# Self-loops counted per node in the setup of a four-layer graph network, and four gathers per tile instead of five

## What is computed

```python
src = concatenate([_s, _d, arange(12500)]); dst = concatenate([_d, _s, arange(12500)])   # then sorted by dst
# layer 0, four steps: a = segment_sum((feat @ W[k].T + b[k])[etype, src], dst); feat = gru(a, feat)
# layer 1, twice:      h = mlp(x + segment_sum(x[src], dst))
# layer 2:             out = segment_sum((x @ W)[src] * deg^-.5[src] * deg^-.5[dst], dst) + b; batch norm
#                      (with one more self-loop per node, added by the layer itself)
# layer 3:             rst = x @ Wself.T + mean over edges of (x[src] * weight) @ Wneigh.T + biases
```

## Time and profile before

| | us |
|---|---|
| median of 3 runs | 9373.61 |
| lowest and highest | 9371.31, 9383.71 |
| the profiled execution | 9385.09 |
| its span, first to last instruction | 9383.3 |
| its mean granted clock | 0.879 |

### The profile page before, as it was taken

The page is one execution under the profiler, slowest core; times in us unless marked ns, Lnnn a source line. Parts: engine busy times, 40 slices in busy tenths (PEclk is TensorE's granted clock), DMA queues, the critical chain, the costliest instruction groups (busy, mean ns, idle before and its releaser), DMA issues.

```text
span 9383.3 us, 311202 instructions
## 1 busy us (share of the span) xinstructions
PE 7002.6 (75%) x128691; PEld 5978.8 (64%) x128692; DVE 7411.2 (79%) x16871; ACT 2629.0 (28%) x6519; POOL 5105.8 (54%) x4469
## 2 busy tenths in 40 slices
PE   3666666668888887887777777756578777748988
PEld 2333333348877887887777676655567766637887
DVE  7888888869988997887888766555567766668998
ACT  0000000013333332333555433311133322224443
POOL 0000000026667776776666588777778867755554
PEclk8887787879999999999999888877888888869999
DMA  3211111147777777777666777777777777748888
GB/s 87 66 46 46 46 47 51 46 130 205 203 209 205 208 207 205 206 203 209 179 176 179 201 211 211 216 217 203 222 214 205 206 225 212 209 117 228 225 225 193
DMA packets 1186021, 1618.18 MB, mean 172 GB/s; under 512 B 421509, under 2 KB 864808, under 8 KB 1181691
## 3 DMA queue, kind: packets, MB, share of 16 engines
q1 hardware_dynamic: 916698, 898.54, 35.7%
q10 hardware_dynamic: 126656, 482.46, 15.0%
q0 software_dynamic: 141280, 217.70, 11.4%
HBM read 1034.03 MB, written 564.09 MB: 170 GB/s over the span
## 4 chain that ended last, share of the span: by engine, by line
issue 32%; DVE 23%; PE 18%; POOL 14%; DMA 7%; DVEq 5%; ACT 1%; SPq 0%; ACTq 0%; POOLq 0%
POOL work L910 14%; DMA work<-node_rows,work 5%; DVE work L1916 4%; DVE work L1891 4%; PE ps_agg L1142 3%; DVE hs L1882 2%; PE ps_pair L1089 2%; PE ps_gate L1186 2%; DVE work L1872 2%; PE ps_agg L1120 1%; PE ps_agg L1122 1%; PE ps_agg L1121 1%; DVE work L1911 1%; DVEq L1898 1%; PE ps_gate L1188 1%
## 5 line engine op out<-in xcount | busy, mean ns | idle before, releaser
L910 POOL DMA_INDIRECT work<-node_rows,work x4410 | 5049.1, 1145 | 2197.8 <-issue 1408.1
L1142 PE MATMUL ps_agg<-work 128*128 128x64 bf16 (+1 forms) x29400 | 1152.6, 197 | 769.4 <-DMA work<-node_rows,work 693.7
L1120 PE MATMUL ps_agg<-work 120*128 120x64 bf16 (+1 forms) x12544 | 1433.2, 201 | 249.4 <-DVE work L1916 241.0
L1142 PEld LDWEIGHTS ps_agg<-work 128*128 128x128 bf16 x29400 | 1039.1, 101 | 825.0 <-issue 753.1
L1121 PE MATMUL ps_agg<-work 120*128 120x64 bf16 x12544 | 1426.9, 201 | 17.6 <-issue 17.3
L1122 PE MATMUL ps_agg<-work 120*128 120x64 bf16 x12544 | 1427.2, 201 | 11.1 <-issue 11.1
L1120 PEld LDWEIGHTS ps_agg<-work 120*128 120x128 bf16 x12544 | 1240.8, 104 | 287.2 <-issue 286.0
L1121 PEld LDWEIGHTS ps_agg<-work 120*128 120x128 bf16 x12544 | 1228.8, 104 | 27.0 <-issue 13.9
L1122 PEld LDWEIGHTS ps_agg<-work 120*128 120x128 bf16 x12544 | 1223.6, 103 | 9.7 <-issue 9.4
L1089 PE MATMUL ps_pair<-rows_now,work 128*128 128x64 bf16 x26112 | 1040.8, 200 | 133.7 <-DMA work<-src_onehots 55.3
L1911 DVE TENSOR_TENSOR work<-work 120x1024 f32<-120x1024 f32 x784 | 955.6, 1219 | 188.1 <-DMA work<-bounce_f 187.7
(11 more groups left out here) (323 smaller groups left out, 12115.4 us busy)
## 6 DMA issues: line engine op xcount, KB each, us to landing
bounce_f<-work ACTq DMA_DIRECT2D x816, 480.0 KB
work<-bounce_f SPq DMA_DIRECT2D x784, 480.0 KB
work<-src_onehots SPq DMA_DIRECT2D x918, 256.0 KB
bounce<-work ACTq DMA_DIRECT2D x102, 727.5 KB
work<-bounce SPq DMA_DIRECT2D x98, 727.5 KB
work<-node_rows,work POOLq DMA_INDIRECT x4410
work<-grid_vals SPq DMA_DIRECT2D x49, 960.0 KB, 5.0
node_rows<-stage SPq DMA_DIRECT2D x686, 48.0 KB
```

Of the source, the lines that this page charges most:

```text
L910: pool.indirect_dma_start(out=ring[:, at.slot3() * LB + b, 0:3 * H], out_offset=None, in_=table_of(at.p), in_offset=bass.IndirectOffsetOnA ...
L1120: mm(acc[:, to:to + n], hot, low[at.two()][0:ROWS, b, 0:n], start=b == 0, stop=False)
L1142: last = mm(acc[:, k * TYPE_W:k * TYPE_W + n], hot, ring[:, u * LB + b, x * H:x * H + n], start=False, stop=end and p < P_GIN1 and k == K ...
```

## The change

Self-loops no longer go into the grid or the left-over batches. In the setup each edge record carries a mark for a self-loop (in `PEN`, negative), and such edges get neither a slot nor a left-over place. GpSimd makes for each of them a row of flags by type, weight and its three parts (`own_fields`); the placing matmul of the left-over rows sums them per node as a fifth record behind four batches (`RECS` = 5 records, `LB` = 4 batches, so the matmul keeps its width of 35), and GpSimd folds the sums (`own_sums`): counts for four types, the sum of weights, and the count plus one. In the passes `take_sums` adds count times own row: in passes 0 to 3 per type, in 4 to 7 with the count plus one (which replaces the identity matmuls), in 8 with the weight sum. SP waits for `sum_taken` before it reloads a record slot or `rows_now`, as both are now read there. GpSimd issues four gathers per tile; their batches are four on TensorE too. In `rank_pair` several pairs of small VectorE instructions become one over both tiles.

```diff
-LB = 5
+LB = 4
 LEFT = LB * P
+RECS = LB + 1
...
         def load_recs(at, more):
+            if not (isinstance(at.i, int) and at.base + more < 6):
+                sp.wait_ge(sum_taken, at.tiles(more - 5))
+                sp.sem_inc(sp_ran, 1)
...
             if p < P_GCN:
                 sp.wait_ge(tile_summed, NT * p + CREDIT_T + 6 * CHUNK)
+                sp.wait_ge(sum_taken, NT * p + 6 * CHUNK)
                 reload(p, 5)
             store_rows(At(p, NT - 1))
             if p < P_GCN:
                 sp.wait_ge(tile_summed, NT * (p + 1) + CREDIT_T)
+                sp.wait_ge(sum_taken, NT * (p + 1))
                 reload(p, 6)
...
+        def own_fields(q, par):
+            two, to = win[par], left_now[:, :, :, LB, :]
+            pool.wait_ge(own_known, q + 1)
+            pool.sem_inc(pool_ran, 1)
+            g.tensor_scalar(own_here, own, 0.0, None, ALU.is_lt)
+            for k in range(K):
+                g.tensor_scalar(own_type[:, :, :, k], two[:, :, :, TYPE], float(k), None, ALU.is_equal)
+            pool.drain()
+            flags = own_here.rearrange("p t (n o) -> p t n o", o=1)
+            g.tensor_tensor(to[:, :, :, 0:K], own_type, flags.to_broadcast([P, 2, WC, K]), ALU.mult)
+            g.tensor_tensor(to[:, :, :, K:LV], two[:, :, :, W0:W2 + 1], flags.to_broadcast([P, 2, WC, LV - K]), ALU.mult
+                            ).then_inc(own_made, 1)
+
+        def own_sums(q):
+            to = left_out[:, :, LB, :]
+            pool.wait_ge(left_copied, q * 2 + 2)
...
+            pool.drain()
+            g.tensor_tensor(own_two, to[:, :, 0:2], to[:, :, 2:4], ALU.add)
+            g.tensor_tensor(own_one[0], to[:, :, K], to[:, :, K + 1], ALU.add)
+            pool.drain()
+            g.tensor_tensor(own_one[1], own_two[:, :, 0], own_two[:, :, 1], ALU.add)
+            g.tensor_tensor(to[:, :, OWN_W], own_one[0], to[:, :, K + 2], ALU.add)
+            pool.drain()
+            g.tensor_scalar(to[:, :, OWN_N], own_one[1], 1.0, None, ALU.add).then_inc(own_mended, 1)
+
+        def own_pair(q, par):
+            for t in range(2):
+                pool.wait_ge(left_placed[t], q)
+            pool.sem_inc(pool_ran, 1)
+            own_fields(q, par)
+            own_sums(q - 1)
...
             pe.wait_ge(left_made, q + 1)
+            pe.wait_ge(own_made, q + 1)
...
-                if end and p >= P_GIN1:
-                    for x in range(3):
-                        last = mm(acc[:, 0:H], eye_bf[:, :],
-                                  rows_now[:, ds(at.d(), 1), x * H:(x + 1) * H].rearrange("p o f -> p (o f)"),
-                                  start=False, stop=x == 2)
...
+            v.tensor_tensor(own_f, src_l[:, at], dst_l[:, at], ALU.is_equal)
...
+            if not first:
+                dve.wait_ge(own_made, q)
+            v.scalar_tensor_tensor(out=own, in0=two[:, :, :, PEN], scalar=0.0, in1=here, op0=ALU.min, op1=ALU.mult
+                                   ).then_inc(own_known, 1)
...
             if at.p < P_GIN1:
                 v.tensor_reduce(out=state[at.half()][:, 0:H],
                                 in_=tile(rows_now, at).rearrange("p (a f) -> p f a", a=3), axis=AX.X, op=ALU.add)
-            elif at.p in (P_GIN2B, P_SAGE):
+            elif at.p < P_SAGE:
+                v.tensor_reduce(out=own_x[at.half()][:, :],
+                                in_=tile(rows_now, at).rearrange("p (a f) -> p f a", a=3), axis=AX.X, op=ALU.add)
+            if at.p in (P_GIN2B, P_SAGE):
                 v.tensor_copy(state[at.half()][:, 0:H], tile(hs if at.p == P_GIN2B else xs, at))
 
         def take_sums(at, careful=False):
             p, acc = at.p, ps_agg[at.half()]
             more = extra[:, at.place(), :]
+            own_rec = lrec[at.slot6()][:, LB, :]
+            if P_GIN1 <= p < P_SAGE:
+                dve.drain()
             dve.wait_ge(tile_summed, at.tiles(CREDIT_T + 1))
             if p < P_GIN1:
...
-                v.tensor_copy(agg_sb[:, :].rearrange("p (k f) -> p k f", k=K), typed[:, :, 0:H])
+                v.tensor_tensor(to, own_rec[:, 0:K].rearrange("p (k o) -> p k o", o=1).to_broadcast([P, K, H]),
+                                state[at.half()][:, 0:H].rearrange("p (o f) -> p o f", o=1).to_broadcast([P, K, H]),
+                                ALU.mult)
+                dve.drain()
+                v.tensor_tensor(to, to, typed[:, :, 0:H], ALU.add)
...
+                    dve.drain()
+                    v.scalar_tensor_tensor(out=to, in0=tile(xs, at), scalar=own_rec[:, OWN_W:OWN_W + 1], in1=to,
+                                           op0=ALU.mult, op1=ALU.add)
                 else:
-                    last = v.tensor_copy(to, acc[:, 0:H])
+                    last = v.scalar_tensor_tensor(out=to, in0=own_x[at.half()][:, :], scalar=own_rec[:, OWN_N:OWN_N + 1],
+                                                  in1=acc[:, 0:H], op0=ALU.mult, op1=ALU.add)
```

More of the change, by code:

```diff
@@ L57 @@
 LV = W2 + 1
+OWN_W, OWN_N = K, LV
 CW = 3 * H + 2
@@ L158, in build @@
     left_ws = [c.take(8 * LB, bf16).rearrange("p (a g) -> p a g", a=4) for _ in range(2)]
-    lrec = [c.take(LB * 8, fp32).rearrange("p (g f) -> p g f", f=8) for _ in range(6)]
+    lrec = [c.take(RECS * 8, fp32).rearrange("p (g f) -> p g f", f=8) for _ in range(6)]
     squares = work[:, 0:NT * H]
@@ L180, in build @@
     s_i, lo_i, dt_i, dl_i, sb_i = [c.take(QC, i32) for _ in range(5)]
-    below96, cls_f, pos_a, pos_b, w_rest = [c.take(QC, fp32) for _ in range(5)]
+    below96, cls_f, pos_a, pos_b, w_rest, own_f, own_at, other = [c.take(QC, fp32) for _ in range(8)]
     w_bf = [c.take(QC, bf16) for _ in range(2)]
@@ L194, in build @@
     earlier = c.take(WC * WC, bf16).rearrange("p (o n m) -> p o n m", o=1, m=WC)
-    here, key, rank, ahead, left, left_sum, spare_pos, batch = [
-        c.take(2 * WC, fp32).rearrange("p (t n) -> p t n", t=2) for _ in range(8)]
+    here, key, rank, ahead, left, left_sum, spare_pos, batch, own, placed, own_here = [
+        c.take(2 * WC, fp32).rearrange("p (t n) -> p t n", t=2) for _ in range(11)]
+    own_type = c.take(2 * WC * K, fp32).rearrange("p (t n k) -> p t n k", t=2, k=K)
+    own_two = c.take(4, fp32).rearrange("p (t k) -> p t k", t=2)
+    own_one = [c.take(2, fp32) for _ in range(2)]
     spare_i, batch_i = [c.take(2 * WC, i32).rearrange("p (t n) -> p t n", t=2) for _ in range(2)]
@@ L1711, in rank_pair @@
             dve.drain()
-            for t in range(2):
-                v.tensor_tensor(key[:, t, :], rank[:, t, :], two[t][:, :, PEN], ALU.add)
+            v.tensor_tensor(key, rank, two[:, :, :, PEN], ALU.add)
             dve.drain()
@@ L1724, in rank_pair @@
             v.tensor_copy(row_total[:, 2:4], wide_col[:, :]).then_inc(totals_made, 1)
-            v.tensor_tensor(spare_pos, left_sum, left, ALU.subtract)
+            v.scalar_tensor_tensor(out=spare_pos, in0=left_sum, scalar=-1.0, in1=left, op0=ALU.add, op1=ALU.mult)
+            v.scalar_tensor_tensor(out=placed, in0=own, scalar=0.0, in1=left, op0=ALU.is_lt, op1=ALU.add)
             def at_place(numbers):
@@ L1755, in rank_pair @@
             v.tensor_copy(batch, batch_i)
-            v.scalar_tensor_tensor(out=spare_pos, in0=spare_i, scalar=1.0, in1=left, op0=ALU.add, op1=ALU.mult)
+            v.scalar_tensor_tensor(out=spare_pos, in0=spare_i, scalar=1.0, in1=placed, op0=ALU.add, op1=ALU.mult)
             dve.drain()
```

82 lines of the change are left out of this document (52 added, 30 removed).

## The result

The changed kernel takes 9071.83 us (median of 4 runs, 9058.99 to 9081.15) against 9378.66 us before on the same chip. The ratio is 0.9671, with a 95% interval of 0.9654 to 0.9688. The forecast was 9050 us, a ratio of 0.9655.

The account below looks back on a forecast made before the run. Passes 4 to 7 bound by issuing gathers, passes 3 and 8 by VectorE; 9385.1 - 347 + 26 - 8 - 2 + 5 = 9059, scaled to 9048, said as 9050 us; range 8930 to 9250 us.

Parts of the forecast that it names:

- Gather issue bounds passes 4 to 7, the excess is the tile's: Passes 4 to 7: 1.25 us per gather plus a fixed excess per tile, 0.95 to 1.47 us; -347 us in all.
- The bare bounds: Passes 4 to 7: GpSimd's work with four gathers plus excess, 6.47, 6.11, 6.42 and 5.95 us per tile.
- The 0.25 to 0.35 us for later transfers: Passes 4, 5 and 7: added per tile for waits on the bounce buffer, giving 6.7, 6.4 and 6.3 us.
- rival A: Passes 4 to 7: transfers become the bound, tiles about 7.2, 7.0, 7.3, 6.9 us, total about 9230; chance 0.2.
- Pass 6: Pass 6: VectorE occupied 6.81 us per tile plus 0.28 waiting for the square root, 7.1 us; gain 0.59.
- Passes 0 to 3: Passes 0 to 3: +0.07 us per tile over 392 tiles, +26 us; removing gathers and matmuls pays nothing.
- The VectorE term of +0.15: Passes 0 to 3: product 0.33 and drain 0.08 less one-hot 0.30, taken as +0.15 us per tile; bounds +0.05, +0.45.
- VectorE's remaining waits shrink: Passes 0 to 3: TensorE loses 0.47 us and GpSimd falls to about 6, so VectorE's waits (0.24 in pass 1) shrink.
- Pass 8: Pass 8, VectorE-bound: narrower tensor_tensors save 0.1 each, own row and drain take 0.31; -0.09 us per tile, -8 us.
- Setup: Setup: VectorE savings -15, record parts +11, last pair's sums +2; together -2 us, bounds -20 and +40.
- rival C: Setup: GpSimd's small instructions meet the shared lock, over 38.8 us per pair; at 50 us, kernel about 9600; chance 0.05.
- The queues: SP's new waits before reloading record slots: covered by its wait for TensorE except at pass ends, +5 us; uncovered +118.

Follow-up runs that it names:

- Experiments 8 to 10: Changed kernel, product on ScalarE and source matmuls moved: 8869.76 us; also pass 6's own row on TensorE, pass 8's on ScalarE: 8805.55; then move only in passes 0, 3: 8808.72.

## Why the prediction was right, and where it was not

**Gather issue bounds passes 4 to 7, the excess is the tile's.** Gather issue bounded all four before the change; right. That the excess is fixed, which the prediction named as a condition of its own success, held in passes 4 and 6 (1.47 to 1.39, 1.42 to 1.41) and not in 5 and 7. The bare bounds were 6.47 and 6.11 us for passes 4 and 5; the tiles are 6.41 and 6.35. In pass 5 the excess rose from 1.11 to 4 x (428.37 / 334 - 0.95) = 1.33, and 5.0 + 1.33 is its tile. With five gathers put back it is 1.33 too, so it isn't the gathers' number that raised it; what did is open. The 6.4 us forecast for pass 5 is met by this and not by the transfers that were added for it, which is luck. GpSimd waits for TensorE only 7.0 us of 590 in pass 4, with gathers back to back:

```profile
POOL work L971 <- issue: 105.2, 345, 0.3
POOL work L971 <- PE ps_agg L1204: 7.0, 23, 0.3
```

**The 0.25 to 0.35 us for later transfers** was too much in passes 4 and 5, where it was nothing. VectorE does wait for the bounce buffer there, 21.4 us in 590 of pass 4, but that is absorbed. DMA ran at a share of 0.90, as worked out (0.91). In pass 7 the tile is 0.09 over the bound of 5.95, but the bound itself went down: the excess there is 4 x (373.17 / 351 - 0.95) = 0.45 and not 0.95, and GpSimd is no longer last. The signs that the prediction named for rival A are in this pass, in 530 us:

```profile
POOL work L971 <- PE ps_agg L1204: 52.3, 24, 3.9
...
DVE work L1977 <- DMA work<-bounce_f: 41.2, 27, 3.7
```

They come at a tile of 6.04 us and not of 6.9. Rival A as priced didn't come in any pass.

**Pass 6** was forecast at 7.1 us and takes 6.89. VectorE is its bound:

```profile
DVE agg_sb L2031 <- issue: 2.7, 6, 0.5
DVE work L1982 <- issue: 2.7, 6, 0.5
```

These are its largest waits in 620 us. The 6.81 of occupied time was right, at 614.6 / 90 = 6.83 (its added terms come to 0.28 and not 0.29, which changes nothing); the wait of 0.28 for the square root, which I kept, went too. Taking VectorE's reduction out (Experiments 8 to 10) brought 0.26.

**Passes 0 to 3** were forecast at +0.07 us per tile; they are +0.17 on average. The VectorE term of +0.15 fits the tiles at the full clock: their median interval in pass 1 went from 7.32 to 7.42 us and in pass 3 from 8.66 to 8.82. In it, two wrong sizes offset each other: the product is busy 161.7 / 392 = 0.41 us, as it overlaps nothing, and not 0.33, and the one-hots fell by 0.34 and not 0.30. The step that failed is "VectorE's remaining waits shrink". I counted the product as occupied time and didn't ask who waits for the instruction behind it, and I booked the loss of twelve matmuls as a gain only. The product and its drain lie on the way from TensorE's sum to TensorE's transposes, so TensorE's pause there grew by 0.49 us. In pass 3 the clock is low in three tiles of four where it was in one of four, and VectorE waits for the gate 0.64 us per tile where it waited 0.19. About half of the added slow tiles go with the product on VectorE; what makes the others is not shown. Pass 0, at 8.09 us per tile against 7.76, has the same marks, weaker (14 lower tiles of 87 against 4). Zeros at the tile's end took away its lower tiles and 0.12 us, and with the product on ScalarE it is at 7.43. That shorter waits would raise the clock held only in pass 4 (0.82 to 0.90) and in passes 6 and 7 (0.86 to 1.00, 0.85 to 0.92), and hardly in pass 5 (0.80 to 0.81).

**Pass 8** was forecast at -0.09 us per tile and is +0.11. Narrower one-hots save 0.07 to 0.08 each and not 0.1 (L1901 went from 0.493 to 0.425), and the own row's instruction takes 0.286 and not 0.23:

```profile
L1967 DVE TENSOR_TENSOR work<-iota_bf,work 128x512 bf16<-128x512 bf16 x490 | 208.5, 425 | 37.5 <-issue 1.3
L2028 DVE SCALAR_TENSOR_TENSOR agg_sb<-xs,work,agg_sb 128x64 f32<-128x64 f32 x98 | 28.0, 286 | 7.5 <-issue 0.4
```

That is -0.30 + 0.29 + 0.08 for the drain, +0.07.

**Setup** came out at -9.7 us, within its bounds. But GpSimd's small instructions take 608.80 / 49 = 12.4 us per pair, twice what I gave them; the 37.8 us from one pair to the next cover it, and rival C is out by that margin. **The queues**: no run isolates what SP's new waits cost. The cover that the prediction counted on is there: in pass 3 SP stands 129.3 us at the new wait (L758), and behind it still 292.9 at the wait for TensorE (L816), where it stood 303.2 before (L800).

## What to carry to other kernels

Count the instructions that a queue issues per unit of work, with their gaps: an engine shown as 80% busy can be full. When a step is added to an engine, cost it twice, once as occupied time and once as delay for the engine that waits for it; here that second engine was TensorE, whose clock changed too. Moving matmuls that are due anyway into the pause was worth 1.1% of the changed kernel, and moving the step to an engine with time left 2.1% (0.9562 and 0.9471 against 0.9671). When two theories each have a run that seems to settle them, look into the other runs for the same mark: the pause was short again in a run made for another purpose, and the clock was still low in half of the tiles.

## What the hardware showed

- A gather that starts under a long VectorE tensor_tensor with both inputs in SBUF waits for its end. In passes 4 to 7 of the changed kernel's trace 790 of 1568 gathers start under one of over 1 us, at least 0.05 us before its end; 757 of them last over 1 us, and those end 0.82 us (nearly all within 0.01) after that instruction. The 778 others last 0.96 us on average, and one of them over 1.1. The prediction's first pair fits: its gather ends at 6428.26, 0.82 us after the end of L1872 at 6427.44. So the excess depends on how early in such an instruction a gather starts, and it differs by pass with that: under the second split (L1982) gathers last 1.82 us in pass 4 and 1.05 in pass 7. The Trainium skill (SBUF — State Buffer, Who interferes with whom) has the lock but leaves tensor_tensor out for descriptor writing, and the prediction took its rows to disagree. The same section says that a VectorE instruction with two SBUF inputs contends with a GpSimd one that reads SBUF. A gather reads its indices from there (`work` in L971's rows), and by that rule the trace agrees.
- The same shows on GpSimd's elementwise work in the setup, where an instruction over four columns once took 3.79 us, the length of VectorE's 6912-column ones: it starts 0.02 us after one and ends 0.05 us after it. From the changed kernel's timeline, GpSimd's and then VectorE's:

```profile
165.29 3.79 POOL L943 TENSOR_TENSOR work<-work 128x4 f32<-128x4 f32 x1 [0.15 <-issue]
...
165.27 3.76 DVE L1744 TENSOR_TENSOR work<-hs,work 128x6912 bf16<-128x6912 bf16 x1 [1.09 <-ACT work L1387]
```

  The TENSOR_SCALARs over 36 columns have a mean of 1.6 us, by its lines:

```profile
L928 POOL TENSOR_SCALAR work<-work 128x36 f32<-128x36 f32 x196 | 306.7, 1622 | 0.0
```

- TensorE's granted clock in pass 3 can't be read off its busy share. At 80% busy it was 0.96 with 24 zeros in the pause (625.15 of 780 us) and 0.88 with 12 at the tile's end (637.68 of 800); at 74% it was 0.92 with the useful matmuls moved (595.99 of 800), and at 77% in the changed kernel 0.87. Nor can it be read off the pause alone: at 1.20 us in front of the transposes it was 0.96 before the change, and at 1.18 us, with the product on ScalarE, 0.89.
